# Exponential ahead of the clip in cross attention, and reciprocals of softmax sums in turned 32x32 blocks

## What is computed

```
# attn0, attn1
probs = softmax(q @ k.T * 32**-0.5, axis=-1);  out = probs @ v

# xattn
scores = q @ k.T / sqrt(32)
scores = clip(scores, -50, 50)
scores = where(attend[:, None, None, :], scores, -10000.0)
scores = clip(scores, -50, 50)                  # a masked key: -50
probs = softmax(scores, axis=-1)
probs = probs / (probs.sum(-1) + 1e-8)
ctx = probs @ v
```

## Time and profile before

| | us |
|---|---|
| median of 3 runs | 2064.85 |
| lowest, highest | 2061.89, 2064.95 |
| profiled execution, its span | 2056.5 |

### The profile page before, as it was taken

How to read it: one execution, slowest core, us unless ns; L and a number is a source line. 1 busy time by engine, 2 the same in 40 slices (tenths; PEclk the granted TensorE clock), 3 DMA queues, 4 the chain that set the end, 5 groups by cost and what they waited for, 6 DMA issues and landing times.

```text
span 2056.5 us, 28429 instructions
## 1 busy us (share of the span) xinstructions
PE 1639.2 (80%) x9252; PEld 640.5 (31%) x9253; DVE 1369.1 (67%) x2092; ACT 854.3 (42%) x1015; POOL 522.9 (25%) x413
## 2 busy tenths in 40 slices
PE   1998898988948935777699899999697887877837
PEld 1323233232336622333323333232232312222213
DVE  3876867858645537999285564738547677666868
ACT  1152240532523315776435353534546262542613
POOL 1514216133120015111401212130232311313117
PEclk9999999999979977998899999999899999898968
DMA  7201103002124444000210202020330110202102
GB/s 284 63 2 36 46 0 80 2 22 60 42 91 143 143 128 62 1 0 0 80 34 3 60 0 61 0 51 10 123 82 21 33 28 20 61 20 51 31 5 82
DMA packets 80843, 106.08 MB, mean 52 GB/s; under 512 B 14112, under 2 KB 51360, under 8 KB 80672
## 3 DMA queue, kind: packets, MB, share of 16 engines
q1 hardware_dynamic: 77216, 97.14, 15.9%
q0 software_dynamic: 3584, 8.39, 2.0%
HBM read 49.26 MB, written 18.35 MB: 33 GB/s over the span
## 4 chain that ended last, share of the span: by engine, by line
PE 35%; issue 25%; DVE 19%; POOL 6%; SPq 5%; ACT 4%; DMA 3%; DVEq 1%; POOLq 0%; ACTq 0%
PE ps L389 13%; PE ps L630 11%; SPq L568 5%; DVE arena L825 5%; PE ps L599 5%; PE ps L729 4%; DVE arena L970 2%; DVE arena L845 2%; POOL arena L1064 2%; DVE stats L171 1%; ACT arena L806 1%; DVE arena L1486 1%; DMA arena<-arena 1%; DVE arena L1497 1%; PE ps L615 1%
## 5 line engine op out<-in xcount | busy, mean ns | idle before, releaser
L630 PE MATMUL ps<-arena 128*32 128x512 f32 x3072 | 399.5, 623 | 45.1 <-ACT arena L806 33.0
L825 DVE TENSOR_REDUCE arena<-ps 128x1 f32<-128x512 f32 x512 | 323.1, 678 | 147.3 <-PE ps L599 146.9
L806 ACT ACTIVATE arena<-ps 128x1024 f32<-128x1024 f32 x256 | 252.1, 1025 | 314.9 <-PE ps L729 313.8
L389 PE MATMUL ps<-xt,w 128*128 128x512 f16 (+1 forms) x1872 | 293.4, 310 | 36.1 <-DVE arena L876 17.9
L729 PE MATMUL ps<-arena 97*128 97x512 f16 (+1 forms) x768 | 216.8, 386 | 19.2 <-DVE arena L970 15.1
L599 PE MATMUL ps<-arena 96*128 96x512 f16 x512 | 186.8, 398 | 53.1 <-DMA arena<-arena 33.9
L389 PEld LDWEIGHTS ps<-xt,w 128*128 128x128 f16 (+1 forms) x1872 | 156.9, 100 | 176.3 <-issue 66.2
L389 PE MATMUL ps<-w,arena 128*128 128x512 f16 (+1 forms) x804 | 180.0, 381 | 12.7 <-issue 12.7
L806 ACT ACTIVATE arena<-arena 128x1024 f32<-128x1024 f32 x128 | 134.0, 1056 | 130.9 <-DVE arena L970 125.1
L970 DVE TENSOR_SCALAR arena<-ps,arena 128x1024 f32<-128x1024 f32 x128 | 157.1, 1256 | 38.4 <-PE ps L729 38.1
L1004 POOL TENSOR_TENSOR arena<-arena 128x512 f32<-128x512 f32 x36 | 57.2, 1589 | 447.3 <-DVE arena L845 447.3
(11 more groups left out here) (171 smaller groups left out, 2089.0 us busy)
## 6 DMA issues: line engine op xcount, KB each, us to landing
arena<-arena SPq DMA_DIRECT2D x576, 64.0 KB, 2.0
raw<-in_ctxT SPq DMA_DIRECT2D x8, 1024.0 KB, 5.4
raw<-in_ffn_parts SPq DMA_DIRECT2D x16, 512.0 KB, 3.5
...
```

What stands on the lines that cost most here:

```text
L389: last = pe.matmul(out, left[l](cl[k]), right[r](cr[k]), start=start and k == 0 and a == 0, stop=stop and k == n - 1 and a == 2)
L630: last = pe.matmul(self.m.ps[HD * j:HD * (j + 1), 7 if ones else 6, :], left, self.pt[:, u % 2, j * S:(j + 1) * S], start=kb == 0, stop=kb ...
L806: act.activation(out, src, ACT.Exp, scale=SOFTMAX_SCALE).then_inc(self.exp_done[h], 1)
L825: v.tensor_reduce(self.mx[:, j:j + 1], self.row_bank(at), AX.X, ALU.max).then_inc(self.row_free[at[0]], 1)
```

## The change

Two things. In xattn the exponential now reads the scores in PSUM, as in the other attentions, and VectorE clips its result in `pt`, in place, between exp(-50) and exp(50) (masked keys: exp(-50)). TensorE waits for `exp_done` before it overwrites the scores' banks and for `clipped` before the values.

And the sums aren't copied by ScalarE. VectorE turns bank 7 in blocks of 32x32 into `sums`. Since the 32 partitions of a head hold the same numbers, each block's first column then holds 32 different ones, one to a partition: 16 columns hold all. It inverts those 16 columns (`inverse`), and turns them back, each column read 32 times over, into `sums`. Each of the three waits for the one before. TensorE waits for the first of them (`sums_read`) as well as for the copy of bank 6 (`ctx_copied`). The whole stands in one piece ahead of kb = 1 of the next group, in all three attentions, and in `dve_last_context` in place of the reciprocal of bank 7.

```
@@ pe_values
-                pe.wait_ge(*self.at(self.exp_done[h], b * NH + u + 1))
+                pe.wait_ge(*self.at((self.clipped if self.cross else self.exp_done)[h], b * NH + u + 1))
             if kb == 0 and g:
-                pe.wait_ge(*self.at(self.ctx_free, (b * (C - 1) + g) * 2))
+                pe.wait_ge(*self.at(self.ctx_free, b * (C - 1) + g))
+                pe.wait_ge(*self.at(self.sums_read, b * C + g))
@@ pe_heads
-                        pe.wait_ge(*self.at((self.clipped if self.cross else self.exp_done)[h], b * NH + u))
+                        pe.wait_ge(*self.at(self.exp_done[h], b * NH + u))
@@ act_context
-        act.activation(self.sums, self.m.ps[:, 7, :], ACT.Copy).then_inc(self.ctx_free, 1)
         act.activation(self.ctxn, self.m.ps[:, 6, :], ACT.Copy).then_inc(self.ctx_free, 1)
@@ act: xattn goes the way of the others
-                    if self.cross:
-                        act.wait_ge(*self.at(self.clipped[h], b * NH + u + 1))
-                        src = out
...
+                    act.wait_ge(*self.at(self.st_full[h], b * NH + u + 1))
+                    act.wait_ge(*self.at(self.pv_done, b * NH + max(u - 1, 0)))
+                    act.activation(self.pt[:, u % 2, 2 * h * S:(2 * h + 2) * S], flat(self.m.ps[:, 2 * h:2 * h + 2, :]),
+                                   ACT.Exp, scale=SOFTMAX_SCALE).then_inc(self.exp_done[h], 1)
@@ dve_invert
-    def dve_invert(self, v, g, k, b):
-        v.wait_ge(*self.at(self.ctx_free, (b * (C - 1) + g) * 2 + 1))
-        part = self.sums[:, k * P:(k + 1) * P]
-        v.reciprocal(part, part).then_inc(self.inverted, 1)
+    def dve_invert(self, v, g, b):
+        v.wait_ge(*self.at(self.pv_done, b * NH + T * (g + 1)))
+        v.wait_ge(*self.at(self.normed, b * C + g))
+        v.transpose(self.sums, self.m.ps[:, 7, :]).then_inc(self.sums_read, 1)
+        v.wait_ge(*self.at(self.sums_read, b * C + g + 1))
+        one = self.inverse.rearrange("p (n k) -> p n k", k=1)
+        v.reciprocal(one, blocked(self.sums)[:, :, 0:1]).then_inc(self.reciprocals, 1)
+        v.wait_ge(*self.at(self.reciprocals, b * C + g + 1))
+        v.transpose(blocked(self.sums), one.broadcast_to([P, NQ, HD])).then_inc(self.inverted, 1)
@@ dve_last_context
-        v.wait_ge(*self.at(self.pv_done, (b + 1) * NH))
+        self.dve_invert(v, g, b)
         v.wait_ge(*self.at(self.cl, b * C + g))
-        v.reciprocal(self.sums, self.m.ps[:, 7, :]).then_inc(self.inverted, 4)
@@ dve_heads
+            if g and kb == 1:
+                self.dve_invert(v, g - 1, b)
             if self.cross:
                 for h in range(2):
-                    v.wait_ge(*self.at(self.st_full[h], b * NH + u + 1))
-                    v.wait_ge(*self.at(self.pv_done, b * NH + max(u - 1, 0)))
-                    v.tensor_scalar(self.pt[:, u % 2, 2 * h * S:(2 * h + 2) * S], flat(m.ps[:, 2 * h:2 * h + 2, :]),
-                                    slot_col(self.hi, b * T + kb), -50.0 / SOFTMAX_SCALE, ALU.min, ALU.max).then_inc(self.clipped[h], 1)
-                    if g and kb in (1, 2):
-                        self.dve_invert(v, g - 1, 2 * (kb - 1) + h, b)
+                    p = self.pt[:, u % 2, 2 * h * S:(2 * h + 2) * S]
+                    v.wait_ge(*self.at(self.exp_done[h], b * NH + u + 1))
+                    v.tensor_scalar(p, p, slot_col(self.hi, b * T + kb), CLIP_LOW, ALU.min, ALU.max).then_inc(self.clipped[h], 1)
...
+def blocked(ap):
+    return ap.rearrange("p (n k) -> p n k", k=HD)
```

More of the change, by code:

```diff
@@ L8 @@
 from contextlib import ExitStack
+import math
 import concourse.bass as bass
@@ L43 @@
 SOFTMAX_SCALE = HD ** -0.5
+CLIP_HIGH, CLIP_LOW = math.exp(50.0), math.exp(-50.0)
+NQ = S // HD
 def tile3(ap):
@@ L427, in __init__ @@
             self.cos, self.sin, self.rot = take(S), take(S), take(P)
-        self.ctxn, self.sums = take(S), take(S)
+        self.ctxn, self.sums, self.inverse = take(S), take(S), take(NQ)
         self.vb, self.ob = take(D), take(D)
@@ L478, in __init__ @@
         self.st_full, self.exp_done = self.sems("scores_full", 2, NB * NH), self.sems("exp_done", 2, NB * NH)
-        self.pv_done, self.ctx_free, self.inverted = s("pv_done", NB * NH), s("ctx_free", NB * (C - 1) * 2), s("sums_inverted", NB * C * 4)
+        self.pv_done, self.ctx_free = s("pv_done", NB * NH), s("ctx_copied", NB * (C - 1))
+        self.sums_read, self.reciprocals, self.inverted = s("sums_read", NB * C), s("reciprocals", NB * C), s("sums_inverted", NB * C)
         self.normed, self.ch, self.cl = (s(n, NB * C) for n in ("ctx_normed", "ctx_high", "ctx_low"))
@@ L532 @@
     WITH_UNIT = [(2, 1, 1, 2, 1), (1, 1, 1, 1, 0), (2, 1, 1, 1, 0), (0, 0, 0, 0, 0)]
-    INVERT = [(), (0, 1), (2,), (3,)]
     def first(self, table, i):
@@ L797, in act @@
                 for h in range(2):
-                    out = self.pt[:, u % 2, 2 * h * S:(2 * h + 2) * S]
-                    if self.cross:
-                        act.wait_ge(*self.at(self.clipped[h], b * NH + u + 1))
-                        src = out
-                    else:
-                        act.wait_ge(*self.at(self.st_full[h], b * NH + u + 1))
-                        act.wait_ge(*self.at(self.pv_done, b * NH + max(u - 1, 0)))
-                        src = flat(self.m.ps[:, 2 * h:2 * h + 2, :])
-                    act.activation(out, src, ACT.Exp, scale=SOFTMAX_SCALE).then_inc(self.exp_done[h], 1)
+                    act.wait_ge(*self.at(self.st_full[h], b * NH + u + 1))
+                    act.wait_ge(*self.at(self.pv_done, b * NH + max(u - 1, 0)))
+                    act.activation(self.pt[:, u % 2, 2 * h * S:(2 * h + 2) * S], flat(self.m.ps[:, 2 * h:2 * h + 2, :]),
+                                   ACT.Exp, scale=SOFTMAX_SCALE).then_inc(self.exp_done[h], 1)
                 if kb == 0 and g:
@@ L868, in dve @@
             v.wait_ge(*self.at(self.consts_done, 2))
-            top = 50.0 / SOFTMAX_SCALE
-            v.tensor_scalar(self.hi, self.mask, 0.5, 2.0 * top, ALU.is_gt, ALU.mult).then_inc(self.consts_done, 1)
+            v.tensor_scalar(self.hi, self.mask, 0.5, CLIP_HIGH - CLIP_LOW, ALU.is_gt, ALU.mult).then_inc(self.consts_done, 1)
             v.tensor_scalar(self.rs, self.rs, 0.0, 0.3, ALU.max, ALU.min).then_inc(self.consts_done, 1)
             v.wait_ge(*self.at(self.consts_done, 4))
-            v.tensor_scalar(self.hi, self.hi, -top, None, ALU.add).then_inc(self.consts_done, 1)
+            v.tensor_scalar(self.hi, self.hi, CLIP_LOW, None, ALU.add).then_inc(self.consts_done, 1)
             v.tensor_scalar(self.rs64, self.rs, 1.0 / WSCALE, None, ALU.mult).then_inc(self.consts_done, 1)
@@ L977, in dve_heads @@
                     self.dve_rowmax(v, g + 1, [j + n], b)
-                    if g and n % 2 and n // 2 < len(self.INVERT[kb]):
-                        self.dve_invert(v, g - 1, self.INVERT[kb][n // 2], b)
                 if kb == T - 1:
                     self.dve_turn_max(v, g + 1, b)
-                    if g:
-                        self.dve_invert(v, g - 1, T - 1, b)
-            elif kb == 1:
-                for n in range(4):
-                    self.dve_invert(v, g - 1, n, b)
             if g == C - 1:
@@ L1000, in pool_context @@
     def pool_context(self, g, c, b):
-        g.wait_ge(*self.at(self.inverted, (b * C + c + 1) * 4))
-        g.wait_ge(*self.at(self.ctx_free, (b * (C - 1) + c + 1) * 2))
+        g.wait_ge(*self.at(self.inverted, b * C + c + 1))
+        g.wait_ge(*self.at(self.ctx_free, b * (C - 1) + c + 1))
         g.tensor_tensor(self.ctxn, self.ctxn, self.sums, ALU.mult).then_inc(self.normed, 1)
```

2 lines of the change are left out of this document (1 added, 1 removed).

## The result

| | before | after |
|---|---|---|
| median of 15 runs each, us | 2062.34 | 2072.98 |
| lowest, highest, us | 2056.90, 2070.04 | 2070.28, 2077.22 |
| ratio, 95% interval | | 1.0046 [1.0036, 1.0056] |
| profiled execution, its span, us | 2056.5 | 2070.4 |
| heads loops of attn0 and attn1, us | 513.3 | 551.4 |

The forecast was +2 us, at 2067, with 2048 to 2088 as its range; the measured difference is +9.5 us by the ratio, and it lies on the slower side of the bound of no change. Both large terms are there and nearly cancel: +38.1 us in attn0 and attn1 (forecast +31.8), -31.1 in cross attention (forecast -30). The other 6.9 us between the two profiled spans lie outside the heads loops.

A forecast was written before the change was run, and what follows sets the result against it. TensorE sets the time in attn0 and attn1; cross attention was bound by clip, exponential and values in sequence. +31.8 us there and -30 in cross attention make +2, added to the median 2064.85: 2067 us, range 2048 to 2088.

The forecast's parts named there:

- block: VectorE's transpose, reciprocal, transpose in one piece ahead of row maximum 8 of the next group: 1.60 us.
- units 5 and 9, attn0 and attn1: Groups 1 and 2: TensorE waits 1.52 us for a row-maximum bank; unit 5 near 5.96 us instead of 4.44.
- unit 6 after a block: Attn0 and attn1: without reciprocals between the maxima, TensorE's wait of 0.27 us shrinks to about 0.1, giving back 0.16.
- unit 13: Attn0 and attn1, group 3: values wait for the sums' transpose behind the turned x, +1.25 us; 4.55 instead of 3.32.
- last context of a batch: VectorE's 3.36 us become 1.69, already hidden behind TensorE's matmuls: gain 0.
- xattn, stall of unit 13: GpSimd's audio subtraction of 4.09 us holds the clip through a shared port; TensorE's values come 3.7 us late.
- xattn, heads loop: Cross attention, one batch: units sum to 56.3 us, plus 5.5 of clock, 61.8 against 69.3 before.
- Rival B: Slower: a 32-bit transpose takes longer than one pass, deciding from about 0.75 us; at 1.26, 2097 us. Chance 0.24.
- Rival C: Faster: transposes at two columns a cycle, 0.48 us, make the block 1.2 in attn0 and attn1; 2056 us. Chance 0.05.
- Rival D: Cross attention's clip stays at one column a cycle, 1.26 us, and GpSimd blocks nothing; about 2055 us. Chance 0.05.
- Rival A: Faster: GpSimd's long subtraction doesn't hold cross attention's clips; 10 to 21 us less, 2046 to 2057. Chance 0.18.
- 5.5 us of clock a batch: Cross attention: granted clock falls, 2.75 us each, behind the audio passes and behind the GpSimd block.

The follow-up runs named there:

- e3: Changed kernel with one more VectorE operation of 512 columns inside the block of attn0 and attn1; 2095.31 us, 1.0159 of before.
- e5: Changed kernel with TensorE's wait for the sums' transpose moved from the values matmuls to the sums' matmuls; 2056.46 us, 0.9960 of before.
- e6: e5 with the block split in three between row maxima (attn0, attn1) and the last group's first transpose ahead of the turned x; 2022.40 us, 0.9786 of before.
- e4: Changed kernel with GpSimd's audio subtraction moved behind its context of group 2, after the cross heads loop; 2051.60 us, 0.9947 of before.
- e2: Kernel before with the turned reciprocals alone, the cross clip still first and from PSUM; 2094.34 us, 1.0145 of before.
- e1: Kernel before with the exponential ahead of the clip alone, sums copied and four reciprocals as before; 2033.83 us, 0.9851 of before.
- e7: e6 with GpSimd's audio subtraction moved behind its context of group 2, as in e4; 2008.65 us, 0.9721 of before.
- e8: e7 with ScalarE's audio passes cut into four pieces, in units 5, 6, 9 and 10 of cross attention; 1992.28 us, 0.9650 of before.

## Why the prediction was right, and where it was off

By its own steps, forecast against measured (us):

| step | forecast | measured |
|---|---|---|
| transpose of 512 columns | 0.69 | 0.71 |
| reciprocal of 16 columns | 0.23 | 0.25 |
| block | 1.60 | 1.66 |
| units 5 and 9, attn0 and attn1 | 5.96 | 6.02 |
| unit 6 after a block | 4.29 - 0.16 | 4.13 |
| unit 13 | 4.55 | 4.55, 4.64 in attn0 |
| heads loop without a clock fall | 68.1 | 68.12 to 68.30 |
| last context of a batch | 0 | hidden |
| xattn, exponential 9 behind unit 8's start | 7.2 | 7.2 |
| xattn, stall of unit 13 | 3.7 | 3.75 |
| xattn, heads loop | 61.8 | 60.6 to 63.0 |

**Right for the reasons given.** The +31.8 us came from TensorE's wait for one row-maximum bank and for bank 7, at the places named; e3 shows that the block is paid in full, e5 and e6 that each wait goes when its cause goes. Rival B (a transpose above 0.75 us) is out: all 96 take 0.70 to 0.72 us. The Trainium skill's 311 ns for 128 columns of 16-bit data (VectorE: DVE Perf Modes, The three transpose paths) had led to an estimate of 0.71; the trace agrees with that estimate, for 512 columns of f32. Rival C is out with it. Rival D is out: the clip went from 1.26 to 0.75 us. Rival A, that the long GpSimd operation doesn't hold a clip, is out by the clip beside L1051 and by e4. The Trainium skill (SBUF — State Buffer, Who interferes with whom) has a VectorE instruction in a 2-port mode and a GpSimd one exclude each other for the whole instruction; by that rule the clip waits out all that is left of a subtraction of 4.08 us, and the trace agrees at that length too. The last context was hidden as counted: behind the last values TensorE has 10.53 us of matmuls, and the transposes and reciprocal are done 1.9 us into them.

```profile
1260.67 10.53 PE L393 MATMUL ps<-w,arena 128*128 128x512 f16 x48
1260.81 0.72 DVE L844 STREAM_TRANSPOSE arena<-ps 128x512 f32<-128x512 f32 x1 [0.56 <-PE ps L634]
1261.56 0.25 DVE L847 RECIPROCAL arena<-arena 128x16 f32<-128x16 f32 x1
1261.85 0.71 DVE L849 STREAM_TRANSPOSE arena<-arena 128x512 f32<-128x512 f32 x1
```

**What the sum left out is the clock, in attn0 and attn1.** That part has no term for it, though the one for xattn does. Of the +38.1 us, 8 x (1.58 + 1.58 - 0.16 - 0.16 + 1.3) = 33 are the waits. Another 4.5 are falls of the granted clock: 6.1 us in three units of this execution (3.1 in a unit 5 and a unit 9, 3.0 in a unit 1), against 1.6 in one unit 1 of before. Unit 5 of attn0, batch 0, where it fell, and batch 1, where it didn't:

```profile
119.49:127.09 7.60, 6.08 (x26) 1.12 (x25) 4.71 (x9) 2.31 (x3) 1.27 (x1) 0.78 0.01 2
257.45:263.47 6.02, 4.50 (x26) 1.03 (x25) 4.72 (x9) 2.31 (x3) 1.27 (x1) 1.00 0.00 0
```

The same 26 matmuls are busy for 6.08 instead of 4.50 us at a mean clock of 0.78 (0.5 is 1.2 GHz, 1.00 is 2.4). That falls in units 5 and 9 come from the new waits is shown by where they occur, and by e3, where a longer wait made them more. In the five kernels whose units 5 and 9 have the wait, the clock falls in 2 of the 16 such units (changed kernel), 7 (e2), 12 (e3, with the longer wait), 2 (e4) and 3 (e5); in the five without it (before, e1, e6, e7, e8) in none of 80. A fall in unit 1 of a batch, of 1.5 to 3.0 us, occurs in kernels of both kinds and says nothing; so 3.1 of the 4.5 us are the change's, and the rest is this execution's. How many of the 16 are hit varies between kernels with the same waits (2 and 7), and which ones can't be foretold from these runs.

**The size of it in cross attention was off the other way.** I took 5.5 us of clock a batch from the 2.75 of the earlier trace rows. An estimate from this trace's units puts a loop without falls at 57.4 (units 0 to 3 11.2, 4 to 7 12.2, 8 to 11 14.8, which is the lowest, 15.7, less 0.9 for values that took 2.83 us instead of 1.93, 12 to 14 13.7 with the stall of 3.75, unit 15 5.5), 1.1 above my 56.3, and the falls are the other 3.2 to 5.6 us, 4.1 in the mean. The two errors cancel to 0.3 us, and that is luck: that a term comes out right doesn't make its parts right.

**The mapping to the median.** I added the +2 to the median of three runs, 2064.85. That of 15 runs of before is 2062.34. And I had put the whole 8.4 us between its span and the median down to what lies around the span; in the kernels after it the time is only 1.8 us above the span of the same execution (e1: 2033.83 and 2032.0), so the profiled execution of before, at 2056.5, would be 2058.3, one of its fastest. With the median of 15 and the same +2 I would have said 2064, 9 us short and not 6: that part of the nearness is luck too. The spans differ by 13.9 us, the ratio of the medians says 9.5, and the heads loops of the two executions +7.0. Of the 6.9 us outside them 6.0 stand behind the last heads loop, where the change touches one context only. These stretches, from the end of the last heads loop to the end, first after, then e4:

```profile
1970.78:2070.40 99.62, 52.91 (x241) 23.17 (x240) 77.31 (x130) 22.49 (x34) 35.74 (x21) 0.74 0.13 45
```

```profile
1952.49:2045.90 93.41, 48.62 (x241) 22.13 (x240) 73.33 (x130) 22.23 (x34) 45.28 (x22) 0.76 0.16 59
```

It is the same code in both, but for the end of GpSimd's audio subtraction, which e4 has moved there, and the same 241 matmuls are busy 4.3 us longer in one. All of the difference lies in the last linear layer, first after, then e4:

```profile
2013.20:2070.40 57.20, 42.44 (x192) 18.62 (x192) 49.14 (x69) 17.04 (x28) 32.62 (x16) 0.79 0.20 74
```

```profile
1994.90:2045.90 51.00, 38.15 (x192) 17.61 (x192) 44.95 (x68) 16.78 (x28) 39.16 (x16) 0.83 0.22 83
```

There the mean granted clock is 0.79 in the long execution and 0.83 in the short one. The ten profiled executions fall in two groups: 93.4 to 94.7 (before, e1, e2, e4) and 99.0 to 99.7 (after, e3, e5 to e8). Since e4 and e2 have the new reciprocals and the short end, and e1 and e4 the new order of clip and exponential, neither part of the change is its cause; what decides which of the two a run takes stays open.
